# Order of the last steps of a graph-attention kernel on one core

## The reference

```python
h = jnp.maximum(_layernorm(x, axis=-1), 0.0)
s_i = h @ attn[:d]
s_j = h @ attn[d:]
e = leaky_relu(s_i + s_j.T, negative_slope=0.2)
e = e + jnp.where(adj > 0, 0.0, -1000000000.0)
x = x + softmax(e, axis=1) @ h
```

## Time and profile before

| what | value |
|---|---|
| median of 3 runs | 815.93 us (812.81 to 816.13) |
| the profiled execution's time | 815.03 us |
| its span in the profile | 813.2 us |
| busy DVE, ACT, POOL, PE | 77%, 66%, 65%, 45% of the span |
| the chain that ended last: DMA, engines waiting for nothing seen, DVE, ACT, PE | 69%, 13%, 8%, 3%, 3% |
| last sign operation ends | 748.2 us |

### The profile page before, as it was taken

One profiled execution on the slowest core, in us unless ns is written; L12 is line 12 of the kernel. 1 busy time (PEld: TensorE's weight loads), 2 busy tenths in 40 slices (PEclk: granted clock), 3 DMA queues, 4 the chain that ended last, 5 costly groups with the idle time before them and its releaser, 6 DMA issues.

```text
span 813.2 us, 6462 instructions
## 1 busy us (share of the span) xinstructions
PE 368.4 (45%) x1380; PEld 163.5 (20%) x1380; DVE 627.4 (77%) x2101; ACT 533.9 (66%) x411; POOL 530.5 (65%) x526
## 2 busy tenths in 40 slices
PE   0554444344443444434434444344344436645652
PEld 0332111111111111111111111111111214423651
DVE  6898379777768667698768776797779899898733
ACT  4985676676766767676666666766766677677330
POOL 6630677755557777756557777676557767777771
PEclk9885655555555555555555555555555655866676
DMA  8999999999999999999999999999999999991110
GB/s 344 401 399 429 385 409 404 410 412 410 412 410 406 409 405 409 407 414 413 413 409 410 404 410 407 408 412 414 411 416 410 405 410 408 406 382 48 43 48 4
DMA packets 39719, 300.22 MB, mean 369 GB/s; under 512 B 10752, under 2 KB 17528, under 8 KB 22272
## 3 DMA queue, kind: packets, MB, share of 16 engines
q1 hardware_dynamic: 24032, 277.04, 83.7%
q0 software_dynamic: 15360, 22.51, 8.1%
q10 hardware_dynamic: 288, 0.26, 0.1%
HBM read 303.76 MB, written 8.98 MB: 385 GB/s over the span
## 4 chain that ended last, share of the span: by engine, by line
DMA 69%; issue 13%; DVE 8%; ACT 3%; PE 3%; POOL 2%; POOLq 0%; ACTq 0%; DVEq 0%
DMA adj_ring<-in_adj_dram 66%; DVE near L779 3%; ACT sign_ring L632 2%; PE words L1515 2%; DMA h_table<-sums 2%; POOL near L539 1%; DVE one_hot L748 1%; DMA near<-h_table,near_id 1%; ACT h_all L644 1%; DVE h_all L784 1%; DMA out_dram<-adj_ring 0%; DVE sums L1047 0%; DVE cand L793 0%; PE words L1511 0%; DVE terms L1042 0%
## 5 line engine op out<-in xcount | busy, mean ns | idle before, releaser
L632 ACT ACTIVATE sign_ring<-adj_ring,half_neg 128x4096 fp8e3<-128x4096 int32 x128 | 474.8, 3710 | 206.5 <-DMA adj_ring<-in_adj_dram 202.0
L539 POOL DMA_INDIRECT near<-h_table,near_id x384 | 416.8, 1085 | 207.6 <-issue 118.3
L1475 PE MATMUL words<-sign_ring,pack_w 128*128 128x512 bf16 x512 | 223.1, 587 | 349.8 <-ACT sign_ring L632 349.8
L793 DVE MAX8 cand<-words 128x8 f32<-128x256 f32 x256 | 91.0, 418 | 97.0 <-PE words L1475 97.0
L1475 PEld LDWEIGHTS words<-sign_ring,pack_w 128*128 128x128 bf16 x512 | 54.5, 126 | 515.5 <-ACT sign_ring L632 446.1
L1047 DVE TENSOR_REDUCE sums<-terms 128x128 f32<-128x1024 f32 x58 | 111.7, 1926 | 2.0
L550 POOL DMA_INDIRECT near_m<-h_table,id_m x64 | 65.1, 1016 | 19.5 <-issue 19.5
L1042 DVE TENSOR_TENSOR terms<-near,weight 128x512 f32<-128x512 f32 (+1 forms) x87 | 72.3, 857 | 0.0
L1466 PE MATMUL words<-place,place_w 128*128 128x512 bf16 x128 | 61.6, 581 | 3.3 <-DVE key L954 3.3
L1501 PEld LDWEIGHTS listing<-cand,one_hot 128*128 128x128 f32 x128 | 32.6, 312 | 11.4 <-issue 7.4
L1456 PE MATMUL listing<-h_all 128*1 128x128 f32 x128 | 20.2, 334 | 25.5 <-ACT h_all L644 25.5
(11 more groups left out here) (293 smaller groups left out, 524.5 us busy)
## 6 DMA issues: line engine op xcount, KB each, us to landing
adj_ring<-in_adj_dram SPq DMA_DIRECT2D x128, 2048.0 KB, 24.4
near<-h_table,near_id POOLq DMA_INDIRECT x384, 6.4
h_table<-h_all POOLq DMA_DIRECT2D x4, 1056.0 KB, 14.9
x_all<-in_x_dram SPq DMA_DIRECT2D x4, 1024.0 KB, 9.4
out_dram<-x_all SPq DMA_DIRECT2D x30, 128.0 KB, 23.5
near_m<-h_table,id_m POOLq DMA_INDIRECT x64
out_dram<-x_all ACTq DMA_DIRECT2D x2, 128.0 KB, 3.0
adj_ring<-h_table SPq DMA_DIRECT2D x1, 132.0 KB, 2.6
```

The costliest lines, as they stand in the source:

```text
L539: pool.indirect_dma_start(out=near[:, p % RING, k, :], out_offset=None, in_=table, in_offset=bass.IndirectOffsetOnAxis(ap=near_id[:, p % I ...
L632: nc.scalar.activation(bytes_of, adj_ring[:, n % HALVES, :].rearrange("p (d r i) -> p d r i", r=2, i=WORDS), ACT.Sign, bias=half_neg[:, :] ...
L793: last = nc.vector.max(out=cand[:, p % 2, t % 2, 8 * q:8 * q + 8], in_=words[t % 3][:, q * PART:(q + 1) * PART])
L1475: last = nc.tensor.matmul(at[:, k * BANK:(k + 1) * BANK], pack_w[:, d, :], twins[:, o + k * BANK:o + (k + 1) * BANK], start=False, stop=(d ...
```

## The change

It computes the same. On ACT the register loads, `exp_pair(BODY + 2)` and its diagonals come before `close_pair(BODY + 1)` and its store, and `exp_lone` after that. On DVE `lone_part` is split: the raw scores of the last lone list (`lone_raw`) stay ahead of `weigh_pair(BODY + 2)`, and the other two operations (`lone_mask`) go behind it; the last lone list's end goes behind the deep sum. On POOL the scatter of lone list 0 goes behind the far loop, and the deep scatter ahead of the last lone list's. The other places of `lone_part` call both halves in turn, as before. PE's and SP's order is the same. Lines behind the split have numbers higher by 6 or 7 in the new text.

```diff
@@ gpsimd
             load_lone(LAST)
-            store_lone(0)
             pool.wait_ge(sizes_ready, 2)
...
+            store_lone(0)
+            store_m(SEGS - 1)
             store_lone(LAST)
-            store_m(SEGS - 1)
@@ scalar
             write_diagonals(BODY + 1)
-            close_pair(BODY + 1)
-            store_pair(BODY + 1)
-            exp_pair(BODY + 2)
             act.wait_ge(sizes_ready, 2)
             tiles = act.value_load(far_tiles[0:1, 0:1], min_val=1, max_val=TILES)
             parts = act.value_load(far_parts[0:1, 0:1], min_val=1, max_val=DC)
+            exp_pair(BODY + 2)
+            write_diagonals(BODY + 2)
+            close_pair(BODY + 1)
+            store_pair(BODY + 1)
             for c in range(LONE_PARTS[LAST]):
                 exp_lone(LAST, c)
-            write_diagonals(BODY + 2)
             close_pair(BODY + 2)
@@ vector
             score_pair(BODY + 2)
-            for c in range(LONE_PARTS[LAST]):
-                lone_part(LAST, c)
+            lone_raw(LAST, 0)
             weigh_pair(BODY + 2)
+            lone_mask(LAST, 0)
...
-            lone_end(LAST)
             score_deep(SEGS - 1)
             add_deep(SEGS - 1)
+            lone_end(LAST)
```

More of the change, by code:

```diff
@@ L1221, in lone_bounds, with lone_raw @@
                 nc.vector.tensor_scalar(lone_max[b], lone_max_leaky[b], MASKED, None, ALU.add).then_inc(lone[b], 1)
-            def lone_part(b, c):
+            def lone_raw(b, c):
                 lt = TILES // LONE_PARTS[b]
@@ L1233, in lone_part, with lone_mask @@
                     .then_inc(lone_masking[b], 1)
+            def lone_mask(b, c):
+                lt = TILES // LONE_PARTS[b]
+                form = [P, lt, LONE_CAP[b]]
+                part = lone_p[b][c % len(lone_p[b])]
+                tiled = part.rearrange("p (t e) -> p t e", e=LONE_CAP[b])
                 dve.wait_ge(lone_masking[b], 2 * c + 1)
@@ L1281, in lone_close @@
                 for c in early_parts(p - FIRST_STEP):
-                    lone_part(0, c)
+                    lone_raw(0, c)
+                    lone_mask(0, c)
             stats_quarter(0)
```

## The result

| | before | after |
|---|---|---|
| median of 4 runs | 815.52 us | 809.69 us |
| lowest and highest | 812.81, 816.13 | 809.09, 811.18 |
| the profiled execution's time | 815.03 us | 809.09 us |
| its span | 813.2 us | 807.2 us |

A fourth run has joined the three of the kernel before, so its median is 815.52 here. The ratio is 0.9945, 95% interval 0.9925 to 0.9965; the medians differ by 5.8 us. The forecast was 808.6, in a range from 806.0 to 812.5. Before and after, the last sign operation ends at about the same time (748.2 and 748.5), so the difference lies behind it: 64.9 us from there to the end before, 58.8 after. Such times are taken from the unrounded trace, so that a difference of printed times can be 0.1 off.

The account below looks back on a forecast made before the run. The tail behind the last sign operation (748.2 to 813.2), a chain of waits between engines, was the bound; an earlier far loop and swapped ends brought the span from 813.2 to 806.8, so 815.03 less 6.4 is 808.6 us, range 806.0 to 812.5.

Parts of the forecast that it names:

- The mix: PE's mix of pair 31 follows pair 30's without a gap, takes 4.1 at the upper clock; transposes at 779.7, not 785.19.
- The rival that the mix stays at the lower clock: PE's last mix takes up to 3.8 more, transposes at 783.5, time 812.4, a gain of 2.6; chance 0.18.
- The rival without a move: Late sizes, loads or another wait keep the far loop in place; only the end swaps gain, time 814.1; chance 0.08.
- POOL's slot: POOL's gathers, 1.0 each and 0.3 apart, run until the slot at 790.30, which the far scatter takes.
- the 3.93: On POOL, the far scatter lands 3.93 after its slot, and the next scatter follows 1.2 behind that.
- The moved scatter: Lone list 0's scatter on POOL, at 795.4, leaves POOL free at 796.8, before the deep sum ends at 797.6.
- The sums of the lone list: PE's lone sums start at 786.6 and ACT's copy comes 4.97 later, at 791.6; bounds 2.7 to 5.3.
- The drain: Rival at POOL's end: 6.4 paid for each scatter under way, two more cost 12.8, time 821.4; chance 0.06.
- the 0.5% that was set as the bound: A change of 0.5%, 4.1 us, is about what a measurement of this kernel can tell from none.

Follow-up runs that it names:

- the gap: The change, but PE waits for the close of pair 30 ahead of the last mix; one run, 809.60 us, ratio not taken.
- The change again: The change itself, unaltered, measured a second time against the kernel before; 807.03 us, ratio 0.9934 (0.9920 to 0.9947).
- mix alone: The change with POOL's scatters and DVE's two ends in the old order, against the kernel before; 807.36 us, ratio 0.9948.
- tail alone: The change with ACT's block and DVE's lone_raw, lone_mask, weigh_pair in the old order, against the kernel before; 810.99 us, ratio 0.9994.

## Why the prediction was right

| step | forecast | measured |
|---|---|---|
| exponential of pair 31 done on ACT | 772.4 | 772.3 |
| diagonals written | 778.8 | 778.4 |
| transposes on PE | 779.7 | 779.3 |
| far loop's first step on DVE | 780.2 | 779.9 |
| far loop's last step done | 788.1 | 787.7 |
| far scatter on POOL | 790.3 | 791.6 |
| lone list 0's scatter | 795.4, for 1.0 | 795.0, for 3.1 |
| ACT's lone copy | 791.6 | 791.8 |
| deep sum done | 797.6 | 797.5 |
| deep scatter | 797.9 | 798.4 |
| last scatter | 799.2 | 799.7 |
| end of the span | 806.8 | 807.2 |

*The mix.* The start, the upper clock and the length held, as the earlier trace rows had it, and the six other profiles with the mix early have the same steps. The rival that the mix stays at the lower clock did not happen in any of the seven profiles in which PE went from one mix to the next; the gap shows 1.3 of its price, with the lower clock for some three microseconds of the mix. The rival without a move fell with the first row.

*POOL's slot.* The far scatter was forecast for 790.3 and came at 791.6. The step that failed is that the gathers stay 1.0 each: two of them, at 772.11 and 774.28, took 1.87 and 1.32:

```profile
772.11 1.87 POOL L550 DMA_INDIRECT near_m<-h_table,id_m  x1 [0.30 <-issue]
774.28 1.32 POOL L550 DMA_INDIRECT near_m<-h_table,id_m  x1 [0.30 <-issue]
```

DVE was at its large lone operations then. But before, the same three operations, from 772.05 on, stood beside gathers of 1.00, so why these two are long is open:

```profile
772.07 1.00 POOL L550 DMA_INDIRECT near_m<-h_table,id_m  x1 [0.30 <-issue]
```

It cost nothing, since the landing was 2.15 instead of the 3.93 that was carried over the earlier trace rows. That the two errors cancel was luck.

*The moved scatter.* That it "costs nothing now only if the deep sum ends later than that" was the condition, and the term of 1.0 in it the one that was mis-sized: 3.08. It made POOL and not the deep sum the last to be ready, and so cost 0.6 (798.36 against 797.77, that is 797.49 and the 0.28 of before).

*The sums of the lone list.* From their start to ACT's copy, 5.67 instead of 4.97, since the clock rose later within them; the bound had been 5.3 at the most. That bound misread, which count a matmul in each window that it touches (the sums' five windows add up to 169, for 128 matmuls). By their starts in the trace of the kernel before, four begin every 0.215 us at the lower clock and every 0.11 at the upper, so that all 128 take an estimated 3.5 to 6.9. The change again, at the lower clock until about 788.4, went well past 5.3:

```profile
783.67 6.00 PE L1568 MATMUL words<-h_all,adj_ring 128*16 128x129 f32 x128
```

*The drain.* From the end of the last scatter to the end of the span there are 6.6 to 6.7 in every profile, be the scatters shortly before one (before, mix alone), two or three (all others). The rival that each is paid for is excluded.

*The size.* The profiled gain was 5.9 for 6.4 forecast. The end came within 0.4 of the forecast although terms on the way were off by 0.7 to 2.1 in both directions, so the mechanism is borne out and so close a number is in part luck. (The lower end of the range, 807.5 less half of 3.3, is 805.8, not 806.0, which changes nothing.) As to the noise, the ratio's interval puts it between 0.35 and 0.75% of the median, which reaches below the 0.5% that was set as the bound, and the second measurement lies between 0.53 and 0.80%.

## What to carry to other kernels

An operation that stands behind a wait on one engine only because the program's text has it there is worth moving as far as its inputs allow, above all where it feeds an engine that else goes idle: the gain was the early start and the clock that PE kept. Look then at what ends last after the change, here POOL's row of gathers and scatters, and put what is ready early (lone list 0) into a slot that nobody waits for, not into the one that just came free at the end. The traces show some 0.6 for that here; it is less than the runs can tell. A small operation carried over at its old price can cost three times as much in a new neighbourhood.

## What was not expected of the hardware

A scatter of POOL beside a run of DVE operations with two tensors in took 3.08, 3.35 and 2.10 instead of 1.0, and ended each time within 0.04 of the end of DVE's run; three others that began earlier in the run took 1.00 to 1.17.

The far scatter landed in 2.14 to 2.19 in the profiles in which POOL had paused 0.30 before it, and in 3.93, 3.60 and 3.13 in those in which POOL had idled 3.14, 4.67 and 2.24 (before, tail alone, gap). Idling alone does not do it: the deep scatter of the kernel before landed in 2.2 behind 5.00 of idle time. What does was not tried.

POOL's own register loads ran from 775.62 to 776.97, with twelve indirect DMAs that stand ahead of them in its list still to run; those stay 0.30 apart, so the loads cost POOL nothing. In all ten profiles the first load starts 0.02 behind the end of an indirect DMA, with just twelve ahead of it still to come: POOL's sequencer ran that far ahead of its work.
